# One core, a fused cross-attention and LoRA-expert kernel: first tile in quarters, gains handled apart, a new order of calls

## The reference

```
q1 = fake_quant(layernorm(x))          # 8 bit, scale and zero point are inputs
q2 = fake_quant(ctx)
x  = x + tanh(g_xattn) * (q1 @ q2)
y  = layernorm(x)
logits = y @ route_w.T                 # 8 experts, the best one is kept
h  = y @ A.T                           # 8 experts x rank 16, only the best one's 16 count
x  = x + tanh(g_ffn) * ((gate * h) @ B.T)
```

## Time and profile before

| what | value |
|---|---|
| median of 3 runs | 363.18 us |
| the profiled execution: span from first to last instruction | 361.7 us |
| runs' median less that span | 1.5 us |
| PE busy | 333.0 us (92%) |
| DVE, ACT, POOL busy | 260.6, 197.4, 172.3 us |
| mean DMA rate | 242 GB/s, 87.63 MB moved |

### The profile page before, as it was taken

One profiled execution on the slowest core, in us unless ns is written; L12 is line 12 of the kernel. 1 busy time (PEld: TensorE's weight loads), 2 busy tenths in 40 slices (PEclk: granted clock), 3 DMA queues, 4 the chain that ended last, 5 costly groups with the idle time before them and its releaser, 6 DMA issues.

```text
span 361.7 us, 5854 instructions
## 1 busy us (share of the span) xinstructions
PE 333.0 (92%) x2237; PEld 186.4 (52%) x2262; DVE 260.6 (72%) x553; ACT 197.4 (55%) x129; POOL 172.3 (48%) x199
## 2 busy tenths in 40 slices
PE   0389999999999999999998999999999999999983
PEld 0244454546756466455464546464464555465751
DVE  3855799898967896958658587945588567585853
ACT  1888489778967262747999270524062413204460
POOL 2559267431265162545999056627064441605281
PEclk9999999999999999999999999999999999999999
DMA  7999999895769998899799996666939890443956
GB/s 301 400 387 404 366 387 380 289 348 173 284 182 212 289 251 291 270 266 294 176 366 157 262 320 121 181 111 177 212 138 158 225 288 31 93 84 59 304 220 232
DMA packets 93906, 87.63 MB, mean 242 GB/s; under 512 B 71844, under 2 KB 72868, under 8 KB 89764
## 3 DMA queue, kind: packets, MB, share of 16 engines
q1 hardware_dynamic: 93856, 87.11, 79.5%
q10 hardware_dynamic: 12, 0.00, 0.0%
HBM read 52.49 MB, written 16.78 MB: 191 GB/s over the span
## 4 chain that ended last, share of the span: by engine, by line
PE 77%; DVE 8%; DMA 7%; issue 2%; ACT 2%; POOL 2%; ACTq 0%; SPq 0%; DVEq 0%
PE main L1575 46%; DMA xs<-in_x 4%; PE hp L1613 4%; PE hp L1617 4%; PE hp L1614 4%; PE outp L1575 4%; PE outp L1658 4%; PE outp L1660 3%; PE outp L1659 3%; DVE bn L971 3%; PE turn L1609 2%; DMA prow<-in_g_ffn 2%; DMA out<-xs 1%; ACT x L753 1%; PE turn L1503 1%
## 5 line engine op out<-in xcount | busy, mean ns | idle before, releaser
L1575 PE MATMUL main<-q,qa 128*128 128x512 bf16 x841 | 194.6, 380 | 5.0 <-POOL q L593 2.3
L1575 PEld LDWEIGHTS main<-q,qa 128*128 128x128 bf16 x864 | 83.2, 98 | 101.2 <-issue 2.7
L586 POOL TENSOR_TENSOR yn<-y,yn 128x2048 f16<-128x2048 f32 x13 | 53.0, 4077 | 31.7 <-ACT y L788 31.7
L735 ACT ACTIVATE c<-stage,zpc,inv 128x2048 int8<-128x2048 f32 x24 | 49.9, 2086 | 7.7 <-DMA stage<-in_ctx 4.0
L593 POOL CAST q<-c 128x2048 bf16<-128x2048 int8 x24 | 45.1, 1893 | 15.3 <-ACT c L735 14.8
L782 ACT ACTIVATE yn<-xs,sc 128x2048 f16<-128x2048 f32 x11 | 23.0, 2093 | 53.4 <-POOL sc L579 49.6
L1104 DVE SCALAR_TENSOR_TENSOR xs<-main,cc,xs 128x512 f32<-128x512 f32 x45 | 33.3, 740 | 21.7 <-PE main L1575 21.5
L574 POOL TENSOR_SCALAR ve<-mv 128x1 f32<-128x1 f32 x16 | 3.1, 191 | 84.8 <-DVE mv L1137 81.8
L1184 DVE SCALAR_TENSOR_TENSOR xs<-outp,tsc,xs 128x512 f32<-128x512 f32 x44 | 31.2, 735 | 13.6 <-PE outp L1660 13.5
L971 DVE BATCH_NORM_STATS2 bn<-xs 128x6 f32<-128x512 f32 x52 | 32.1, 680 | 10.6 <-DMA xs<-in_x 10.6
L753 ACT ACTIVATE x<-xs,sc 128x2048 int8<-128x2048 f32 x12 | 25.0, 2087 | 24.5 <-POOL sc L566 24.4
(11 more groups left out here) (132 smaller groups left out, 435.2 us busy)
## 6 DMA issues: line engine op xcount, KB each, us to landing
stage<-in_ctx SPq DMA_DIRECT2D x24, 1024.0 KB, 7.9
xs<-in_x SPq DMA_DIRECT2D x13, 1024.0 KB, 6.5
out<-xs SPq DMA_DIRECT2D x12, 1024.0 KB, 5.0
yT<-in_ctx SPq DMA_DIRECT2D x4, 1024.0 KB, 9.2
y<-in_ctx SPq DMA_DIRECT2D x4, 1024.0 KB, 10.1
c<-in_x SPq DMA_DIRECT2D x3, 1024.0 KB, 7.4
out<-c SPq DMA_DIRECT2D x3, 1024.0 KB, 7.3
c<-in_L_ffn_A SPq DMA_DIRECT2D x1, 1024.0 KB, 11.5
```

Source lines behind the costliest of these rows:

```text
L586: pool.tensor_tensor(yn[:, 1, :], y[:, :], yn[:, 0, :], ALU.subtract).then_inc(s_ylo_made, 1)
L735: act.activation(c8_of(piece), place(piece), ACT.Identity, bias=zpc[:, 1:2], scale=inv[:, 1:2])\
L1575: last = pe.matmul(bank_of(n)[:, :], q1T(t)[:, k, :], q2[:, nb, k, :], start=(k == 0), stop=(k == KC - 1))
```

## The change

Tile 0's load becomes four loads of 512 columns, each with a semaphore of its own; its statistics wait for each quarter. The two gains are counted, spread (a second small matmul, into `hp`) and copied apart from the four other scalars; tanh moves behind the first half of context piece 0 on ACT, and the constants made of it move on DVE behind tile 0's casts. Piece 0 is made 8-bit and widened in two halves, and the first main run waits for the first half, its third matmul for the second. Every engine's list of calls is in a new order. The core of the diff:

```diff
+            def load_first(q):
+                c0, c1 = q * NW, (q + 1) * NW
+                sp.dma_start(xcol(0, c0, c1), x_t[0][:, c0:c1]).then_inc(s_x_first[q], 16)
...
-            load_x(0)
+            load_first(2)
+            load_first(0)
+            load_first(3)
+            load_first(1)
             load_x(1)
             load_ctx(0)
+            load_x(2)
             load_ctx(1)
-            load_x(2)
+            load_ctx(4)
             load_ctx(2)
             load_ctx(3)
-            load_ctx(4)
+            load_x(3)
             load_ctx(5)
             load_ctx(6)
             load_ctx(7)
-            load_x(3)
+            load_router()
             load_a()
-            load_router()
+            load_ctx(11)
             load_ctx(8)
...
+            def widen_c0(half):
+                c0, c1 = half * 2 * NW, (half + 1) * 2 * NW
+                pool.wait_ge(s_ctx_affine if half else s_c0_half, 1)
+                pool.tensor_copy(in_q2(0)[:, c0:c1], c8_of(0)[:, c0:c1]).then_inc(s_ctx_ready if half else s_c0_wide, 1)
...
-            act.wait_ge(s_par_copied, 1)
-            act.activation(th[:, :], par[:, 4:6], ACT.Tanh).then_inc(s_tanh_done, 1)
+            def tanh_gains():
+                act.wait_ge(s_gains_copied, 1)
+                act.activation(th[:, :], par[:, 4:6], ACT.Tanh).then_inc(s_tanh_done, 1)
...
             affine_first(0)
+            affine_c0(0)
+            tanh_gains()
+            affine_c0(1)
             affine_first(1)
-            affine_ctx(0)
             affine_x(1)
...
+            def stats_first():
+                for nb in range(NB):
+                    dve.wait_ge(s_x_first[nb], 16)
+                    dve.bn_stats(bn1[:, 0, nb, :], xcol(0, nb * NW, (nb + 1) * NW)).then_inc(s_bn1_done, 1)
...
+            stats1(1)
+            take_gains()
             widen_first(0)
+            stats1(2)
             widen_first(1)
+            make_constants()
             take_q1T(0, 0)
             take_q1T(0, 1)
...
+                if n == 0 and run == 0:
+                    pe.wait_ge(s_c0_wide, 1)
+                elif t < G or t == TB:
                     wait_piece(t // TB, nb, run)
                 for k in range(4 * run, 4 * run + 4):
+                    if n == 0 and k == 2:
+                        wait_piece(0, 0, 0)
...
             turn_q1(0, 0)
             turn_q1(0, 1)
             main(0, 0, 0)
             turn_q1(1, 0)
             turn_q1(1, 1)
-            main(0, 0, 1)
             main(1, 0, 0)
             main(1, 0, 1)
```

More of the change, by code:

```diff
@@ L741, in widen_ctx, with affine_c0 @@
                 act.activation(in_q2(piece), c8_of(piece), ACT.Copy).then_inc(s_ctx_ready_act, 1)
+            def affine_c0(half):
+                c0, c1 = half * 2 * NW, (half + 1) * 2 * NW
+                act.wait_ge(landed(0)[0], landed(0)[1])
+                act.activation(c8_of(0)[:, c0:c1], place(0)[:, c0:c1], ACT.Identity, bias=zpc[:, 1:2], scale=inv[:, 1:2])\
+                   .then_inc(s_ctx_affine if half else s_c0_half, 1)
             def affine_first(half):
@@ L1438, in _ @@
             add_experts(10, 2)
+            add_main(13, 0)
+            gate(11)
+            add_main(13, 1)
             add_main(13, 2)
+            add_experts(10, 3)
             add_main(13, 3)
@@ L1481, in _ @@
             pe.wait_ge(s_ones_made, 1)
-            pe.wait_ge(s_par_loaded, 16 * 6)
-            pe.matmul(outp[0][:, 0:6], onesf[0:1, :], prow[0:1, 0:6], start=True, stop=True).then_inc(s_par_spread, 1)
+            pe.wait_ge(s_par_loaded, 16 * 4)
+            pe.matmul(outp[0][:, 0:4], onesf[0:1, :], prow[0:1, 0:4], start=True, stop=True).then_inc(s_par_spread, 1)
             pe.wait_ge(s_flag_ready, 1)
@@ L1493, in wait_turn, with spread_gains @@
                     pe.wait_ge(s, count)
+            def spread_gains():
+                pe.wait_ge(s_gains_loaded, 32)
+                pe.matmul(hp[:, 0:2], onesf[0:1, :], prow[0:1, 4:6], start=True, stop=True).then_inc(s_gains_spread, 1)
             def turn_q1(t, half):
@@ L1706, in _ @@
+            main(0, 1, 3)
             main(3, 0, 1)
             main(3, 0, 2)
-            main(3, 1, 2)
-            column_sums(3, [0])
+            main(1, 1, 3)
+            main(2, 1, 2)
+            main(2, 1, 3)
             main(3, 0, 3)
             column_sums(3, [1])
+            main(3, 1, 0)
+            turn_a(0)
+            main(3, 1, 1)
+            main(3, 1, 2)
+            column_sums(0, [2])
             main(3, 1, 3)
+            turn_a(1)
             turn_a(2)
-            column_sums(0, [2])
@@ L1734, in _ @@
             main(3, 2, 2)
-            main(3, 2, 3)
+            main(1, 2, 2)
+            turn_router()
+            main(0, 2, 2)
+            main(0, 2, 3)
+            main(1, 2, 3)
+            main(2, 2, 1)
             turn_b(0)
             turn_b(1)
-            column_sums(0, [3])
+            main(2, 2, 2)
+            main(2, 2, 3)
+            main(1, 3, 0)
+            main(3, 2, 3)
+            turn_b(2)
+            turn_b(3)
+            column_sums(3, [2])
             main(0, 3, 0)
             main(0, 3, 1)
-            turn_b(2)
-            turn_b(3)
+            column_sums(0, [3])
+            column_sums(1, [3])
+            column_sums(2, [3])
+            column_sums(3, [3])
+            turn_q1(4, 0)
+            turn_q1(4, 1)
             main(0, 3, 2)
             main(0, 3, 3)
-            column_sums(1, [3])
-            main(1, 3, 0)
             main(1, 3, 1)
@@ L1861, in _ @@
             turn_q1(7, 0)
+            expert_product(4, 2)
+            expert_product(4, 3)
+            h_rows_high(5)
+            h_rows_low(5)
             turn_q1(7, 1)
-            h_rows_high(5)
-            expert_product(4, 0)
-            expert_product(4, 1)
-            column_sums(7, range(NB))
             main(7, 0, 0)
-            h_rows_low(5)
-            main(7, 1, 0)
-            main(7, 1, 1)
             main(7, 0, 1)
@@ L1894, in _ @@
             main(8, 1, 0)
+            expert_product(5, 1)
+            column_sums(8, range(NB))
             main(8, 1, 1)
+            main(8, 1, 2)
+            h_rows_high(6)
             main(8, 0, 2)
             main(8, 0, 3)
-            main(8, 1, 2)
+            expert_product(5, 2)
+            h_rows_low(6)
             main(8, 1, 3)
@@ L1928, in _ @@
             main(9, 2, 1)
+            main(9, 2, 2)
+            h_rows_high(8)
+            expert_product(7, 0)
+            expert_product(7, 1)
             main(9, 3, 0)
-            main(9, 2, 2)
             main(9, 2, 3)
```

734 lines of the change are left out of this document (359 added, 375 removed).

## The result

The change makes the kernel slower: 370.3 us as the median of 4 runs (368.43 to 373.26) against 363.35 of the kernel before (4 runs, 363.01 to 363.57), a ratio of 1.0185, 95% interval 1.0151 to 1.022. The runs also lie 4.8 us apart where those of before lie 0.6 apart. The profiled execution took 368.76 us, with a span of 367.0 instead of 361.7.

A forecast was written before the change was run, and what follows sets the result against it. TensorE was taken to bound the kernel, busy 333.0 of 361.7 us. Span 361.7-2.25 (up to 94 us)-0.7 (middle)+0.4 (tail) = 359.15, plus 1.5 to the median: 360.6 us, range 358.4 to 363.9.

The forecast's parts named there:

- the quarters: Start, tile 0 loaded in four parts: its mean 0.6 us earlier, bounds 1.9 earlier to 0.5 later.
- the middle: After 94 us: tile 9's stop near 190 goes (-1.6 us), 0.9 of new waits; net -0.7.
- The table load: Start, ACT: the load moves behind the wait for the first norm, adding 1.28 us to ACT's chain; DVE's wait covers it.
- The first main matmul: Start, TensorE: at 18.5 instead of 16.95, behind tile 2's landing at 13.5 and its statistics; 1.55 us later.
- What the late start gives back: First main matmul to 94 us: 5.3 us lost become 1.5; net up to 94 us -2.25.
- The tail: End of the kernel, reordered y turns and products: 0.4 us later, bounds -0.3 to 1.0.
- The dry queue: Rival, up to 94 us: loads queue behind SP's three waits, DMA runs dry, 6.4 us lost; 365.5 or 364.6; chance 0.15.
- The stops that only move: Rival: 3.7 us of new waits replace those removed up to 94, another 0.7 after; 363.1 us; chance 0.15.

The follow-up runs named there:

- start mended: The changed kernel with tile 0 loaded whole and a tanh of a constant column as ACT's first instruction: 366.52 us, ratio to before 1.0056.
- short stores: Stores of tiles 0 to 10 write only 512 of 2048 columns: changed kernel with whole tile 0 and early table load 361.35 us; kernel before 362.73 us.
- four calls: Kernel before with two expert products of tile 4 earlier on TensorE and two of their additions earlier on VectorE: 362.62 us against 363.94, ratio 0.9963.

## Why the prediction was wrong, step by step

**Where the sum was off.** The forecast span was 359.15, the measured one is 367.0. Of the 7.85 us between them 2.93 arise at the first main matmul (21.43 instead of 18.5), 5.16 between the first and the last one (0.66 more than before instead of 4.5 less), and -0.24 in the tail. Two steps failed, the quarters and the middle.

**The quarters: the step that failed first.** I had the mean of tile 0 come 0.6 us earlier, with 0.5 later as the far bound. It came at 10.80 instead of 8.13: 2.7 later. I counted how many statistics wait for the last quarter, took the four transfers to land when the one did, and allowed 0.5 us for three more issues in SP's queue. They land 3.3 us later in the changed kernel, 3.0 in the kernel before with quarters alone; the three issues by themselves took 1.50 us of it (1.90 for four, 0.40 for one). The Trainium skill, "DMA: Bandwidth & Descriptors", section Anatomy of one DMA, fits a fixed 2.0 us and bytes/436e3 to a transfer issued from GpSimd; SP issues here. By that, which is an estimate, a quarter asked for near 2.2 would land near 4.8; the trace has 8.88, so the fit does not carry over to four in a row from SP, and the trace decides.

**The table load** came where I put it, right ahead of ACT's first half tile, and costs 0.51 us of its 1.28 at the first main matmul once tile 0 is whole. The drain of 1380 ns that the Trainium skill, "ScalarE: Activation LUTs", section What ACT_TABLE_LOAD costs, adds to the load is not in the trace: the load ends at 14.16, the ACTIVATE starts at 14.18.

**The first main matmul.** 18.5 was forecast by way of tile 2 landing at 13.5. In the changed kernel tile 2 is waited for until 16.57 and the matmul comes at 21.43. With tile 0 whole it comes at 18.76, tile 2 is there by 13.4 to 13.6, and VectorE's chain runs as I had added it up. So the rest of this sum stands; the quarters were its error, 2.67 us.

**What the late start gives back.** From the first main matmul to 94 us I had 5.3 us of loss become 1.5. In the stretches of the earlier trace rows the visible part went from 4.15 (4.77 less the 0.62 ahead of the matmul) to 1.1 (1.42 less 0.33). This step was right in the main, 3.05 us of visible idle saved where I had 3.8 with the hidden part: tile 3's statistics run at 30.80 instead of 36.20, and tile 4's main products begin at 91.60 instead of 93.82 in spite of the late start. With tile 0 whole and the first main matmul at 18.76, 1.91 us are idle from there to 94, so the delay by the quarters is not what saves them.

**The middle: the second step that failed.** Net -0.7 was forecast, with 0.9 of new waits. Tile 9's stop did go: 180 to 220 has no idle left. But the four new stops shown above are 4.57 us where I had 0.9 of new waits: idle from 94 to 340 rose from 2.69 to 4.70, and to 9.02 with the start mended (whole tile, early table load). I had bounded the new waits by how little the old order idles (1.06 in 206 us). That is a property of the old order and says nothing of the new one. SP's list of calls would have told it: in the new order the x load stands behind the store it needs, with at most a context piece between, six times instead of two. With short stores the new order takes 315.08 from the first to the end of the last main matmul, 4.0 less than the kernel before. That is near the 4.5 (3.8+0.7) of the forecast, but the old order with short stores takes 317.78: like against like, the new order wins 2.7. It is not bad by itself; it asks more of the stores than they give.

**The tail** was put at +0.4 and is +0.16.

**The rivals.** The dry queue had its first wait: SP stood 12.3 us for the second half of piece 0 and the DMA share from 14.4 to 21.1 fell to 0.69 from 1.04. But TensorE lost far less than the 3.75 us up to 94 from which that case was to decide. It ended on the slower side, by another mechanism than this one. The stops that only move had their second part, new waits in the middle, though larger, and not their first, 3.7 us up to 94. By its own terms this rival's price is 363.55 and not 363.1; the tail's 0.4 seems to be left out.

**What stays open.** The changed kernel's medians lie above its profiled execution (370.3 against 368.76), and its runs spread over 4.8 us. Short stores took 2.0 of 5.1 us from the spread of the kernel with the mended start; what makes the rest, and what makes that of the changed kernel, is open. The tails of the profiled executions differ by 2.0 us (24.58 to 26.62), and in some the granted clock falls: in the changed kernel it is 0.74 as a mean of 360 to 367, between its two levels of 1.2 and 2.4 GHz; from 359.4 the last expert products take 0.63 us instead of 0.38, after TensorE had stood 1.96 us for VectorE. Which of this varies from run to run was not measured.

## What to carry to other kernels

Splitting a transfer so that its first part can be used early pays only if the last part does not come later: look when the last one lands, and at how many are waited for. Where a buffer goes round (store, load into the same home, use), look in the new order for loads that stand right behind their store on the same queue. In this kernel the six cost SP up to 5.6 us each, at tile 3 the transposes behind were held by it, and the slack in that circle, not the idle time of the bound engine, set how much the order could be tightened. Moving the loads behind the transposes was no cure: it made the circle longer (426 us). And a hand-written order on several engines is changed in the few calls that one measured stop names (four calls: -1.3 us); blocks of another order set into it cost 9 to 34 us.

## What the runs showed of the hardware

- One 1 MB load of 128 x 2048, issued by SP in 0.40 us, lands at 5.62; the same megabyte as four of 128 x 512, issued in 1.90, at 8.59 to 8.88, as four of 32 x 2048, issued in 1.81, at 7.42.
- A transpose by DMA holds SP until it is done (118.88 for 6.84 us, the next one goes out at 125.76). Between 100 and 300 us most took 1.6 to 3.4 us, some 4 to 9.3. Three long ones moved ahead of the x load behind which they stood went from 8.62 to 5.15, from 5.41 to 2.86 and from 7.09 to 7.93; with stores of a quarter of the bytes two of them went from 8.62 to 9.25 and from 7.09 to 5.43. What sets the length was not separated.
- In one run VectorE's first small constant took 0.99 us instead of 0.10 and a half cast 1.06 instead of 0.69 while GpSimd was casting; a pair of instructions in one trace, so the cause is not shown.
